# A graph layer with residual and layer norm: groups of 384 nodes with one run of 256 edges instead of groups of 512 with three windows

## The reference

```
msg = relu(x[src] + edge_attr)                      # 25000 x 128
agg = segment_sum(msg, dst, 50000)                  # add each message to its target node
h   = x + agg
h   = relu(h @ W1 + b1) @ W2 + b2                   # 128 -> 256 -> 128, float32
h   = relu(h)
z   = x + h
out = (z - mean(z)) / sqrt(var(z) + 1e-5)           # over the 128 features
```

## Time and profile before

| | before |
|---|---|
| device time, median of 3 (range) | 476.2 us (475.65 to 476.36) |
| span of the profiled execution | 508.3 us |
| time of the profiled execution around its span | not recorded |
| PE busy | 469.2 us (92%) |
| DVE, ACT, POOL busy | 409.9, 399.9, 320.8 us |
| granted TensorE clock, mean | 0.991 |
| DMA | 90.89 MB, mean 179 GB/s |

### The profile page before, as it was taken

How to read it: one execution, slowest core, us unless ns; L and a number is a source line. 1 busy time by engine, 2 the same in 40 slices (tenths; PEclk the granted TensorE clock), 3 DMA queues, 4 the chain that set the end, 5 groups by cost and what they waited for, 6 DMA issues and landing times.

```text
span 508.3 us, 9923 instructions
## 1 busy us (share of the span) xinstructions
PE 469.2 (92%) x2959; PEld 360.2 (71%) x2959; DVE 409.9 (81%) x1539; ACT 399.9 (79%) x881; POOL 320.8 (63%) x315
## 2 busy tenths in 40 slices
PE   5879999999989999989998989989899989989994
PEld 3647777676776777767786767767677867767773
DVE  6567879788797887977887877878778878878885
ACT  2328988797888898877887877878778878878885
POOL 7566766666756676666766656656566666666713
PEclk9979999999999999999999999999999999999999
DMA  5644656655656566655666656657556666656613
GB/s 134 168 135 155 193 185 201 196 175 184 195 173 190 183 206 203 177 174 177 195 199 181 192 173 184 186 172 204 170 183 186 202 182 182 203 173 188 218 58 117
DMA packets 81930, 90.89 MB, mean 179 GB/s; under 512 B 13841, under 2 KB 52372, under 8 KB 81876
## 3 DMA queue, kind: packets, MB, share of 16 engines
q1 hardware_dynamic: 71874, 70.80, 43.3%
q0 software_dynamic: 9728, 19.46, 16.6%
q10 hardware_dynamic: 274, 0.00, 0.0%
HBM read 64.61 MB, written 25.60 MB: 177 GB/s over the span
## 4 chain that ended last, share of the span: by engine, by line
PE 87%; issue 5%; ACT 3%; DVE 2%; another core or an unknown queue 2%; DMA 1%; POOL 0%; SPq 0%; DVEq 0%
PE h_ps L867 33%; PE h1T_ps L859 32%; PE hT_ps L834 13%; PE hT_ps L812 8%; ACT h1T L730 1%; ACT y L749 1%; ACT hT L724 1%; DMA dst_next<-in_dst_dram 1%; ACT msg_hi L718 0%; DVE stats L608 0%; DVE z L601 0%; DVE h L589 0%; DVE before_in_row L288 0%; DVE row_holds L358 0%
## 5 line engine op out<-in xcount | busy, mean ns | idle before, releaser
L109 POOL DMA_INDIRECT x_src<-in_x_dram,src_of x287 | 306.5, 1068 | 165.7 <-ACT hT L724 91.6
L867 PE MATMUL h_ps<-w_sb,h1T 128*128 128x128 f32 x1564 | 195.3, 278 | 3.2 <-ACT h1T L730 3.1
L867 PEld LDWEIGHTS h_ps<-w_sb,h1T 128*128 128x128 f32 x1564 | 183.7, 193 | 5.0 <-ACT h1T L730 4.9
L859 PE MATMUL h1T_ps<-hT,w_sb 128*128 128x512 f32 x392 | 185.7, 596 | 1.6 <-ACT hT L724 1.1
L730 ACT ACTIVATE h1T<-h1T_ps,b_sb 128x512 f32<-128x512 f32 x196 | 128.8, 680 | 55.6 <-PE h1T_ps L859 30.8
L749 ACT ACTIVATE y<-z,shift,rstd 128x128 f32<-128x128 f32 x382 | 165.6, 481 | 1.4 <-DVE shift L628 1.3
L589 DVE TENSOR_TENSOR h<-h_ps,b_sb 128x512 f32<-128x512 f32 x98 | 67.4, 688 | 81.9 <-remote 37.6
L859 PEld LDWEIGHTS h1T_ps<-hT,w_sb 128*128 128x128 f32 x392 | 67.5, 192 | 49.3 <-issue 47.7
L834 PE MATMUL hT_ps<-sel,msg_hi 128*128 128x168 f32 (+1 forms) x281 | 72.9, 293 | 20.8 <-issue 20.8
L608 DVE BATCH_NORM_STATS2 stats<-z 128x6 f32<-128x128 f32 x391 | 85.3, 281 | 0.0
L812 PEld LDWEIGHTS hT_ps<-ident,x_sb 128*128 128x128 f32 (+1 forms) x375 | 46.9, 141 | 50.0 <-issue 49.6
(11 more groups left out here) (115 smaller groups left out, 121.2 us busy)
## 6 DMA issues: line engine op xcount, KB each, us to landing
x_sb<-in_x_dram SPq DMA_DIRECT2D x97, 256.0 KB
out_dram<-y SPq DMA_DIRECT2D x97, 256.0 KB
pre_msg<-in_edge_attr_dram SPq DMA_DIRECT2D x292, 64.0 KB
x_src<-in_x_dram,src_of POOLq DMA_INDIRECT x287
w_sb<-in_w_dram SPq DMA_DIRECT2D x2, 128.0 KB
x_sb<-in_x_dram SPq DMA_DIRECT2D x1, 168.0 KB
out_dram<-y SPq DMA_DIRECT2D x1, 168.0 KB
dst_rows<-in_dst_dram SPq DMA_DIRECT2D x1, 97.7 KB
```

Source lines behind the costliest of these rows:

```text
L109: nc.gpsimd.indirect_dma_start(out=c["x_src"][:, g % EB, k, :], out_offset=None, in_=x, in_offset=bass.IndirectOffsetOnAxis(ap=c["src_of"] ...
L859: nc.tensor.matmul(h1T_ps[h][:, 0:n, 0:p], w1_sb[:, h * 128:(h + 1) * 128], hT[:, 0:n, 0:p], start=True, stop=True).then_inc(h1_summed, 1)
L867: last = nc.tensor.matmul(h2_ps[g % 2][0:p, t, :], h1T[:, h, t, 0:p], w2_sb[:, h, :], start=(h == 0 and t == 0), stop=(h == HC - 1), skip_ ...
```

## The change

Groups of G = 384 nodes (T = 3): 130 full groups and a last one of 80 nodes in one tile, 131 groups. Each group has one run of 256 edges that starts 128 edges before the group's split at node 216 (at most 128 behind its first edge), read as K = 2 chunks of 128: the first may go to positions 0 to 71, the second to positions 56 to 127 (`LO = [0, 56]`, `WP = 72`). The last full group (`END`) has wider chunks, and the last group takes the last 128 edges of the list. Both chunks of `edge_attr` come with one DMA of one start. The lead-in finds one start for a group in place of three, with fewer marks, counts, window gathers and transposes, and only for the groups from 2 on. Groups 0 and 1 take chunks 0 to 3. `GATHER_AHEAD` is 4. The order of the first loads changes (first pairs ahead of the first targets on ACT's queue; more pairs ahead of `dst_next`, w2 and b2 behind the x of group 1 on SP's). In the end POOL normalizes 4 tiles in place of 8.

```
-T = 4
+T = 3
 G = 128 * T
-P0 = [0, 44, 86, 128]
-K = len(P0) - 1
+K = 2
+SPLIT = 72
+LO = [0, 56]
+WP = 72
+END_LO, END_WP = 32, 96
+FIRST_ROW = 2
+LP, LT = 80, 1
-GATHER_AHEAD = 3
+GATHER_AHEAD = 4
-FIRST_CHUNKS = 5
+FIRST_CHUNKS = 4
+PARTS = {g: [slice(0, 1), slice(1, 2)] for g in range(4)}
+WHOLE = {0: 0, 2: 1, 3: 2}
...
+def start_edge_attr(sp, edge_attr, g, first, c):
+    n = windows(g, c)
+    sp.dma_start(c["pre_msg"][:, g % EB, 0:n, :],
+                 edge_attr[bass.ds(first, n * EW), :].rearrange("(k p) d -> p k d", p=EW)).then_inc(c["ea_loaded"][g % EB], 16)
...
+def turn_windows(nc, pe, src_ps, dst_ps, c):
+    R = c["R"]
+    pe.wait_ge(c["window_loaded"], 16)
+    for a, ps, ready in ((0, src_ps, c["src_T_ready"]), (1, dst_ps, c["dst_T_ready"])):
+        for k in range(K):
+            last = nc.tensor.transpose(ps[:, k, :], c["window"][:, k * EW:(k + 1) * EW, a], c["ident"][0:R, 0:R])
+        last.then_inc(ready, 1)
...
     def prepare_sync(sp):
         sp.dma_start(dst_rows[:, :], dst.rearrange("(r e) -> r e", e=ROW)).then_inc(dst_loaded, 16)
+        sp.dma_start(first_pairs[:, 1:FIRST_CHUNKS, :], pairs[EW:FIRST_CHUNKS * EW, :].rearrange("(k p) a -> p k a", p=EW),
+                     allow_slow_non_contiguous=True).then_inc(more_pairs_loaded, 16)
         sp.wait_ge(next_cleared, 1)
...
+        sp.wait_ge(c["first_loaded"][0], 16)
+        start_edge_attr(sp, edge_attr, 1, K * EW, c)
         start_x(sp, x, 1, 1, c)
...
-        for i, k in enumerate(ORDER):
-            count_before(dve, k, i)
-            nc.vector.scalar_tensor_tensor(window_start_i[:, k:k + 1], found_ps[k][:, 0:1], in_row[:, k:k + 1],
-                                           last_window[:, :], ALU.add, ALU.min).then_inc(start_ready, 1)
+        for k in range(K):
+            count_before(dve, k, k)
+        link(dve, first_edge(0))
+        link(dve, nc.vector.tensor_scalar(first_split[:, :], edge_start[:, 0:1], float(EW), float(LAST_WINDOW + EW), ALU.add, ALU.min))
+        link(dve, nc.vector.scalar_tensor_tensor(split[:, :], found_ps[1][:, 0:1], in_row[:, 1:2], first_split[:, :], ALU.add, ALU.min))
+        nc.vector.tensor_scalar(window_start_i[:, :], split[:, :], -float(EW), 0.0, ALU.add, ALU.max).then_inc(start_ready, 1)
...
     def main_gpsimd(pool):
-        pool.wait_ge(c["start_ready"], K)
-        start_window(nc, pairs, 0, c)
+        pool.wait_ge(c["src_of_ready"], 1)
         for g in (2, 3):
-            for i, ks in enumerate(parts(g, c)):
-                for k in range(ks.start, ks.stop):
-                    if g == 2:
-                        pool.wait_ge(c["src_of_ready"], ORDER.index(k) + 1)
-                    start_gather(nc, x, g, k, c["first_loaded"][2 * g + i], c)
+            for k in range(K):
+                start_gather(nc, x, g, k, c["first_loaded"][2 * g + k], c)
...
-        for g, first in ((LAST - 2, 0), (LAST - 1, ACT_TILES)):
+        for g, ts in ((LAST - 2, range(T)), (END, (1,))):
```

456 lines of the change are left out of this document (222 added, 234 removed).

## The result

The changed kernel takes 471.7 us (median of 4 runs, 470.44 to 472.85) where the kernel before takes 476.3 on the same chip: ratio 0.990, 95% interval 0.988 to 0.992, a gain of 4.6 us. The forecast was 465.0, a gain of 11.3. The direction and the steady state were right. The size was more than twice too large: 6.7 us are missing.

What follows compares the result with a forecast made beforehand. PE was taken as the bound (busy 92% of the span), DVE next. Steady part -5.2, lead-in with first periods -3.9 and tail -2.2 sum to -11.3 us, from 476.2 to 465 us; range 459 to 475.

Steps and rivals of the forecast that it cites:

- Steady part: PE's undisturbed periods: 130 groups of 3.40 us in place of 97 of 4.61, -5.2 us.
- the products at 0.11: PE's message products: 216 columns take 0.11 us each from start to start, as 168 do; bounds 0.11 and 0.13.
- DVE as the bound: Rival, add_bias to add_edge_attr on DVE: 0.02 us more per instruction makes periods about 3.52, 480.5 us; chance 0.10.
- the general path: Rival: the windows don't fit and 200 serial tiles run after the fast path, over 1,000 us; chance 0.01.
- So I take no wait for PE: Steady period: msg_lo and hT are ready 0.44 and 0.7 us before PE needs them, so PE never waits.
- First hidden block: Lead-in: window gather issued 1.4 us earlier, so PE's first hidden block starts 1.1 us earlier, bounds 0 and 2.
- First periods: First four periods: 1.1 us more than steady ones where before was put at 4; -2.8 us, bounds 0 and -5.
- Tail: Last hidden block to the last store's issue: 4.65 us in place of 6.87, -2.2 us, bounds -1 and -3.
- lead-in and tail give nearly nothing: Rival: only the steady -5.2 us, or with 1 to 2 of the rest, 470 to 472 us; chance 0.20.

Runs made afterwards that it cites:

- e1: The changed kernel with PE's sum of the check flags one group later (group 31 instead of 30): 469.18 us, ratio 0.9855 to before.
- e2: The changed kernel with the new check of the targets left out: 469.15 us, ratio 0.9853 to before.
- e3: The changed kernel with PE's sum of the flags between the two halves of group 30's output products: 470.43 us, ratio 0.988 to before.
- f4: e1 with the second chunk of groups 2 and 3 summed as two halves, not one whole fp32 product: 478.29 us where before takes 507.81.
- g3: f4 once more, without a further edit: 478.52 us where before takes 508.75.
- h1: f4 plus eight small PE products in the lead-in, the window turned behind the first hidden block, gathers three groups ahead: 474.53 us where before takes 529.18.

## Why the prediction was wrong, step by step

**Steady part: right.** Forecast 3.40 a group, measured 3.407; -5.2 against -4.6, of which 0.9 is that 0.007 and 0.3 the other way is 4.613 for 4.61. DVE's durations, its idle time of 0.22 (0.14 to 0.24 forecast), and the products at 0.11 held. The rivals of DVE as the bound and of the general path did not happen in any of the runs whose trace I have.

**The check behind group 29: not in the sum at all (+3.6).** The failed step is "So I take no wait for PE". It was worked out for a steady period alone. The diff has a new function `check_targets` at the end of DVE's round of group 29, and `sum_flags` on PE waits for two flags where it waited for one. Nowhere did I ask who stands behind this added wait. On DVE the four instructions come behind `add_edge_attr`, the last work of its round; on PE the sum stands ahead of all 12 output products, which need nothing of the check. The rows of before carry the bound: in the undisturbed group DVE's last instruction starts at 191.74 while PE's output block starts at 190.72, so whatever is put behind it holds PE for more than a microsecond. e1 and e2 show the cause. The trace of the changed kernel and e3's show that the second half of the price is the clock, where it falls; in two of four executions it didn't, and the price there was 1.3 to 1.9 us.

**First hidden block (-1.1 forecast, +0.1 measured).** The failed step: "I take 1.1 us for PE's first hidden block" from a window gather issued 1.4 us earlier. The issue was 1.05 earlier, and it waited for DVE's chain of small instructions; the landing took some 2 us longer, which I hadn't priced ("is twice as wide" stands in the prediction without a cost). I also took the window to be the only chain. PE's own one, from `window_start` at 8.4 (8.3 in before) to the hidden block, is 5.8 us long and 5.7 in before. And 13.41, from which I started, is an early one: the same kernel had 14.03 in its second trace.

**First periods (-2.8 forecast, -0.6 measured).** Two sizes were off. (My own terms, 4.15 + 3.7 - 6.8 - 4, give -2.95; the -2.8 is a slip of 0.15.) What before loses in them is 2.98 and not 4: I read the 4 out of an execution that isn't like the median. And the changed kernel loses 2.42 and not 1.1: 0.64 in period 0 (forecast 0.75), but 1.00 in period 1 (forecast 0.3) and 0.38 and 0.39 in periods 2 and 3, where I had put nothing. The whole products don't explain these: group 3's stands in period 2, period 3 has none and loses as much, and taking both out (f4, g3, h1) saved nothing. What sets periods 2 and 3 in the first set stays open.

**Tail: right.** -1.9 for -2.2, to the end of the span. From the last hidden block to the last store's issue, which is what I forecast, it is 468.26 - 462.96 = 5.30 where I had 4.65; in before it is 6.87 again, so -1.6, within the bounds.

The time fell into my range (459 to 475) and near the rival "lead-in and tail give nearly nothing" (470 to 472), but by luck and not by its mechanism: the lead-in did give little, but the tail gave most of what was forecast, and the largest loss was a term that no case of mine had. Without that term (e1) the gain is 7.1 us of the 11.3.

## What to carry to other kernels

Read the once-only instructions of a diff as carefully as the loop. A wait of PE on work at the end of another engine's round costs the distance between the two places, and it can cost nearly the same again if the clock falls behind it, as it did here in some executions; if nothing needs the result soon, put the consumer one round later.

Price a transfer by its landing and not by its issue, and look at what else the DMA engines carry then. Before speeding up one chain of a lead-in, find the others that end at the same time. And compare the profiled execution with the median before taking losses from it: periods that the median can't contain belong in no sum.
